# Output stage of an attention and expert kernel: projections of 64 positions, 8 KB rows for x1 and out, three variances of four on ACT

## The reference

```python
probs = jax.nn.softmax(h @ Wg, axis=-1)            # 16 experts
_, idx = jax.lax.top_k(scores, cap)                # cap = 2 of the 32 tokens at a position, per expert
hg = jnp.take_along_axis(h[:, None, :, :], idx[..., None], axis=2)
q, k, v = ...                                      # of hg, per expert, DH = 64
p = jax.nn.softmax(att, axis=1)
av = jnp.einsum('hbij,hbjd->hbid', p, v)
ao = jnp.einsum('hbid,hde->hbie', av, Wo) + bo
outs = jnp.zeros_like(t).at[b_ids, tok].add(ao)
y = t + outs
mu, var = jnp.mean(y, axis=-1), jnp.var(y, axis=-1)
yn = (y - mu) * jax.lax.rsqrt(var + 1e-05) * ln_g + ln_b
return x1 + yn
```

## Time and profile before

| | us |
|---|---|
| median of 3 runs | 1848.42 (1848.01 to 1849.35) |
| the profiled execution | 1850.22 |
| its span, first to last instruction | 1848.4 |
| busy in the span: PE, DVE, POOL, ACT | 1628.8, 1423.9, 1262.8, 1138.2 |
| output stage on DVE, first addition to last finish | 1457.0 to 1841.8 |
| DMA in and out of the output stage | 1 MB each way for each group |

### The profile page before, as it was taken

The page is one execution under the profiler, slowest core; times in us unless marked ns, Lnnn a source line. Parts: engine busy times, 40 slices in busy tenths (PEclk is TensorE's granted clock), DMA queues, the critical chain, the costliest instruction groups (busy, mean ns, idle before and its releaser), DMA issues. The chain is left out here.

```text
span 1848.4 us, 60029 instructions
## 1 busy us (share of the span) xinstructions
PE 1628.8 (88%) x22957; PEld 1335.7 (72%) x23085; DVE 1423.9 (77%) x3039; ACT 1138.2 (62%) x2758; POOL 1262.8 (68%) x1235
## 2 busy tenths in 40 slices
PE   4899999999999999999999986899997998888993
PEld 3777777777777777777777774899996765556661
DVE  2578788788787787787787877587755399999998
ACT  3677777777777777777777764223322566656662
POOL 1577776776777767767777776578872468776664
PEclk9899999999999999999999998899998799989997
DMA  6122323232232322323222112745653167776886
GB/s 213 52 89 94 99 88 105 88 99 93 93 99 88 103 90 91 102 88 105 88 93 99 48 37 76 253 133 158 199 145 75 34 164 168 171 183 152 196 197 164
DMA packets 106603, 217.83 MB, mean 118 GB/s; under 512 B 13136, under 2 KB 14544, under 8 KB 105552
## 3 DMA queue, kind: packets, MB, share of 16 engines
q1 hardware_dynamic: 96080, 180.42, 33.9%
q0 software_dynamic: 10240, 33.56, 6.2%
HBM read 146.82 MB, written 67.11 MB: 116 GB/s over the span
## 5 line engine op out<-in xcount | busy, mean ns | idle before, releaser
L316 POOL TENSOR_TENSOR rec_hn<-rec_hn,rec_out_w 128x512 f32<-128x512 f32 x128 | 199.5, 1559 | 180.3 <-DVE rec_hn L743 180.3
L294 POOL TENSOR_TENSOR rec_hrs<-rec_harg,rec_minus_half 128x8 f32<-128x8 f32 x128 | 253.8, 1983 | 10.0
L1309 POOL TENSOR_TENSOR out_x_half<-out_x_half,ln_b 128x512 f32<-128x512 f32 x128 | 158.6, 1271 | 117.7 <-DVE out_z_half L1461 117.7
L1409 PE MATMUL out_z_ps<-out_ao,out_hot 128*128 128x512 f32 x256 | 149.5, 668 | 49.3 <-DVE out_z_half L1461 43.7
L1004 PE MATMUL exp_q_ps<-exp_wqkv,exp_rows_t 128*128 128x192 f32 x1024 | 178.1, 327 | 0.1
L709 DVE TENSOR_TENSOR rec_c<-rec_s_ps,rec_d 128x512 f32<-128x512 f32 x256 | 164.7, 685 | 16.4 <-PE rec_s_ps L424 16.4
L540 ACT ACTIVATE rec_d<-rec_l_ps 128x512 f32<-128x512 f32 x256 | 150.4, 587 | 41.5 <-PE rec_l_ps L448 41.1
L1004 PEld LDWEIGHTS exp_q_ps<-exp_wqkv,exp_rows_t 128*128 128x128 f32 x1024 | 166.4, 191 | 0.7 <-ACT exp_rows_t L1058 0.3
L1058 ACT ACTIVATE exp_rows_t<-exp_t_ps 128x512 f32<-128x512 f32 x128 | 69.4, 594 | 157.3 <-PE exp_t_ps L992 132.2
L955 POOL DMA_INDIRECT exp_x_rows<-x_scratch,rowid x128 | 135.0, 1055 | 45.3 <-issue 26.1
L763 DVE TENSOR_TENSOR rec_x_ring<-rec_x_ring,rec_hn 128x512 f32<-128x512 f32 x128 | 88.6, 692 | 100.2 <-POOL rec_hn L316 99.8
(11 more groups left out here) (204 smaller groups left out, 4443.5 us busy)
## 6 DMA issues: line engine op xcount, KB each, us to landing
rec_x_ring<-in_x SPq DMA_DIRECT2D x128, 256.0 KB, 2.7
rec_ctx_ring<-in_ctx SPq DMA_DIRECT2D x128, 256.0 KB, 2.9
x_scratch<-rec_x_ring SPq DMA_DIRECT2D x128, 256.0 KB, 2.0
out_x_half<-x_scratch SPq DMA_DIRECT2D x128, 256.0 KB, 5.6
out<-out_x_half SPq DMA_DIRECT2D x128, 256.0 KB, 3.8
exp_wqkv<-in_wqkv SPq DMA_DIRECT2D x4, 1536.0 KB, 7.4
exp_x_rows<-x_scratch,rowid POOLq DMA_INDIRECT x128
wo<-in_wo SPq DMA_DIRECT2D x1, 2048.0 KB
```

The costliest lines, as they stand in the source:

```text
L294: nc.gpsimd.tensor_tensor(hrs[:, G % 2], harg[:, G % 2], mhalf[:], ALU.pow).then_inc(hrs_done, 1)
L316: nc.gpsimd.tensor_tensor(h, h, w8[:], ALU.mult).then_inc(hw_done, 1)
L1309: nc.gpsimd.tensor_tensor(xt[H % XR][:, q, :], xt[H % XR][:, q, :], lb[:], ALU.add).then_inc(xb_done, 1)
L1409: nc.tensor.matmul(z_ps[T % 3][:], hot[T % 4][:], ao[T % 4][:], start=True, stop=True).then_inc(z_full, 1)
```

## The change

- A projection piece covers 64 positions and half of the heads (`POS = 64`, pieces (k, g)): 8 matmuls of 128 columns instead of 16 of 64. `aot` holds 64 positions. `LEAD` grows from 10 to 18, so nine pieces stand ahead of the first rows. `z_ps` lends its banks to four of the first eight pieces instead of two.
- Positions in a group are numbered (b j t), t fastest: a partition's four tiles are 8 KB in one piece in DRAM. The transposes of av write their columns in that order (a step of 4 columns), and `by_row` reads the identity so.
- Of the four tiles in a group, three (`ON_ACT = 3`) get their sum with the addition (scalar_tensor_tensor with accumulating output, L1496 of the changed kernel), two small DVE operations make the mean (L1503, L1504), and ACT makes the variance: Square with accumulating output over (mean - z)/sqrt(E), L1378. The fourth tile keeps bn_stats and bn_aggr.
- On DVE the scalings of group H move behind the additions of H + 1, ahead of finish(H). z gets two buffers (`ZR = 2`), `ao` lives in the memory of `probs_all`.
- POOL waits for the squares before variance + eps; attend parts stand one group earlier, with two of them in group 0.

The diff, cut to its core:

```diff
-    NBLK = z.S // 32
+    POS = 64
+    PIECES = 2 * KC * z.S // POS
     TILES = z.S // 4
     HALVES = TILES // 4
-    XR, ZR, LEAD = 4, 3, 10
+    XR, ZR, LEAD, ON_ACT = 4, 2, 18, 3
...
-    aot = [sb(f"ao_t{p}", [P, KC, 32, 2 * NE]) for p in range(2)]
-    ao = [sb(f"ao{p}", [P, E]) for p in range(4)]
+    aot = [sb(f"ao_t{p}", [P, KC, POS, 2 * NE]) for p in range(2)]
+    ao = [spare[:, p].rearrange("p h b -> p (h b)") for p in range(4)]
...
     zt = [sb(f"z_half{r}", [P, 4, E]) for r in range(ZR)]
+    dump = sb("squares", [P, E])
+    sums = [sb(f"sums{r}", [P, ON_ACT]) for r in range(2)]
+    offs = [sb(f"offsets{r}", [P, ON_ACT]) for r in range(2)]
...
-    x_view = x1_dram.rearrange("n (b t j) e -> b j n t e", t=4, j=4)
-    o_view = out.rearrange("n (b t j) e -> b j n t e", t=4, j=4)
+    x_view = x1_dram.rearrange("n (b j t) e -> b j n t e", t=4, j=4)
+    o_view = out.rearrange("n (b j t) e -> b j n t e", t=4, j=4)
...
-            pool.wait_ge(agg_done, 4 * H + 4)
+            pool.wait_ge(agg_done, (4 - ON_ACT) * (H + 1))
+            pool.wait_ge(square_done, ON_ACT * (H + 1))
             nc.gpsimd.tensor_tensor(ve[H % 2][:], agg[H % 2][:, :, 1], epsv[:, 4 * H:4 * H + 4], ALU.add).then_inc(ve_done, 1)
             nc.gpsimd.tensor_tensor(rs[H % 2][:], ve[H % 2][:], mhalf[:], ALU.pow).then_inc(rs_done, 1)
-            c, n = divmod(H + 2, 8)
+            c, n = divmod(H + 3, 8)
+            if H == 0:
+                attend(1, 2)
             if n < 4 and c + 1 < NC:
                 attend(c + 1, n)
...
     def projected(u):
-        return z_ps if u in (1, 3) else p_ps
+        return z_ps if u < 8 and u % 2 else p_ps
...
         def put_projection(u):
-            B, k = divmod(u, 4)
+            S, piece = divmod(u, 8)
+            k, g = divmod(piece, 2)
             act.wait_ge(p_full, u + 1)
-            if B >= 2:
-                act.wait_ge(r_full, 8 * (B - 1))
+            if S >= 2:
+                act.wait_ge(r_full, 16 * (S - 1))
             for e in range(2):
-                nc.scalar.activation(aot[B % 2][:, k].rearrange("p b (h e i) -> p b h e i", e=2, i=2)[:, :, :, e, :],
-                                     projected(u)[e][:].rearrange("p (h i b) -> p b h i", i=2, b=32), ACT.Identity,
-                                     bias=bo[:, k:k + 1]).then_inc(p_read, 1)
+                nc.scalar.activation(
+                    aot[S % 2][:, k].rearrange("p b (h e i) -> p b h e i", e=2, i=2)[:, :, 4 * g:4 * g + 4, e, :],
+                    projected(u)[e][:].rearrange("p (h i b) -> p b h i", i=2, b=POS), ACT.Identity,
+                    bias=bo[:, k:k + 1]).then_inc(p_read, 1)
...
+        def deviations(H):
+            for q in range(ON_ACT):
+                act.wait_ge(mean_done, H + 1)
+                if H or q:
+                    act.wait_ge(square_done, ON_ACT * H + q)
+                nc.scalar.activation(dump[:], zt[H % ZR][:, q, :], ACT.Square, bias=offs[H % 2][:, q:q + 1],
+                                     scale=-E ** -0.5, accum_out=agg[H % 2][:, q, 1:2]).then_inc(square_done, 1)
...
         for T in range(-LEAD, TILES):
-            if T % 2 == 0 and T + LEAD < 8 * NBLK:
+            if T > 0 and T % 4 == 0:
+                deviations(T // 4 - 1)
+            if T % 2 == 0 and T + LEAD < 2 * PIECES:
                 put_projection((T + LEAD) // 2)
             if 0 <= T + 2 < TILES:
                 put_rows(T + 2)
-            if T >= 0 and T % 32 in (4, 8, 12, 16) and T // 32 + 1 < NC:
-                put_sums(4 * (T // 32 + 1) + T % 32 // 4 - 1)
+            if T >= 0 and T % 32 in (0, 4, 8, 12) and T // 32 + 1 < NC:
+                put_sums(4 * (T // 32 + 1) + T % 32 // 4)
             if 0 <= T + 4 < TILES:
                 mark(T + 4)
+        deviations(HALVES - 1)
...
-                mm = nc.tensor.transpose(t_ps[:, m * P:(m + 1) * P],
+                by_tile = t_ps[:, m * P:(m + 1) * P].rearrange("p (b t j) -> p b j t", t=4, j=4)
+                mm = nc.tensor.transpose(by_tile,
                                          av[k % 2][:, 2 * m:2 * m + 2, :].rearrange("p h d -> p (h d)"), ident[:])
             mm.then_inc(at_full, 1)
         def project(u):
-            B, k = divmod(u, 4)
-            c, b = divmod(B, 4)
+            S, piece = divmod(u, 8)
+            k, g = divmod(piece, 2)
+            c, b = divmod(S, 2)
             if u % 16 == 0:
                 pe.wait_ge(at_read, 4 * (c + 1))
-            after(pe, p_read, 2 * (u - 1) if u < 4 else 2 * u)
-            for hp in range(HP):
+            after(pe, p_read, 2 * (u - 1) if u < 8 else 2 * u)
+            for hp in range(4 * g, 4 * g + 4):
                 for e in range(2):
                     r = slice(DH * e, DH * (e + 1))
-                    mm = nc.tensor.matmul(projected(u)[e][:, 64 * hp:64 * hp + 64], wo[r, hp, P * k:P * k + P],
-                                          avt[c % 2][r, hp, :, 32 * b:32 * b + 32], start=True, stop=True)
+                    o = (hp - 4 * g) * P
+                    mm = nc.tensor.matmul(projected(u)[e][:, o:o + P], wo[r, hp, P * k:P * k + P],
+                                          avt[c % 2][r, hp, :, POS * b:POS * b + POS], start=True, stop=True)
             mm.then_inc(p_full, 1)
...
-            if T % 2 == 0 and T + LEAD < 8 * NBLK:
+            if T % 2 == 0 and T + LEAD < 2 * PIECES:
-            if T >= 0 and T % 32 in (4, 8, 12, 16) and T // 32 + 1 < NC:
-                sums_by_head(4 * (T // 32 + 1) + T % 32 // 4 - 1)
+            if T >= 0 and T % 32 in (0, 4, 8, 12) and T // 32 + 1 < NC:
+                sums_by_head(4 * (T // 32 + 1) + T % 32 // 4)
...
+        def scale(H):
+            dve.wait_ge(agg_done, (4 - ON_ACT) * (H + 1))
+            dve.wait_ge(mean_link, H + 1)
+            dve.wait_ge(square_done, ON_ACT * (H + 1))
+            for q in range(4):
+                vec.scalar_tensor_tensor(zt[H % ZR][:, q, :], zt[H % ZR][:, q, :], agg[H % 2][:, q, 0:1], lg[:],
+                                         ALU.subtract, ALU.mult).then_inc(zg_done, 1)
+
...
-                vec.tensor_tensor(zt[H % ZR][:, q, :], z_ps[T % 3][:], xt[H % XR][:, q, :], ALU.add).then_inc(z_read, 1)
-            for q in range(4):
+                if q < ON_ACT:
+                    vec.scalar_tensor_tensor(zt[H % ZR][:, q, :], z_ps[T % 3][:], 1.0, xt[H % XR][:, q, :], ALU.mult, ALU.add,
+                                             accum_out=sums[s][:, q:q + 1]).then_inc(z_read, 1)
+                else:
+                    vec.tensor_tensor(zt[H % ZR][:, q, :], z_ps[T % 3][:], xt[H % XR][:, q, :], ALU.add).then_inc(z_read, 1)
+            dve.wait_ge(z_read, 4 * H + ON_ACT)
+            if H >= 2:
+                dve.wait_ge(square_done, ON_ACT * (H - 1))
+            vec.tensor_scalar(offs[s][:], sums[s][:], E ** -1.5, None, ALU.mult).then_inc(mean_done, 1)
+            vec.tensor_scalar(agg[s][:, 0:ON_ACT, 0], sums[s][:], 1.0 / E, None, ALU.mult).then_inc(mean_link, 1)
+            for q in range(ON_ACT, 4):
                 dve.wait_ge(z_read, 4 * H + q + 1)
                 vec.bn_stats(stat[s][:, q, :], zt[H % ZR][:, q, :]).then_inc(stat_done, 1)
-            for q in range(4):
-                dve.wait_ge(stat_done, 4 * H + q + 1)
+            for q in range(ON_ACT, 4):
+                dve.wait_ge(stat_done, (4 - ON_ACT) * H + q - ON_ACT + 1)
                 vec.bn_aggr(agg[s][:, q, :], stat[s][:, q, :]).then_inc(agg_done, 1)
             if H:
+                scale(H - 1)
                 finish(H - 1)
-            dve.wait_ge(agg_done, 4 * H + 4)
-            for q in range(4):
-                vec.scalar_tensor_tensor(zt[H % ZR][:, q, :], zt[H % ZR][:, q, :], agg[s][:, q, 0:1], lg[:],
-                                         ALU.subtract, ALU.mult).then_inc(zg_done, 1)
+        scale(HALVES - 1)
         finish(HALVES - 1)
```

20 lines of the change are left out of this document (11 added, 9 removed).

## The result

| | before | changed |
|---|---|---|
| median, us | 1849.99 (12 runs) | 1844.9 (12 runs) |
| ratio | | 0.997, interval 0.9957 to 0.9983 |
| the profiled execution | 1850.22 | 1843.14 |
| its span | 1848.4 | 1841.3 |

The change makes the kernel 0.3% faster, a little under half of the 0.64% that was forecast. 1844.9 lies in the range and 8.3 us above the point. A second measurement of the same kernel gave 0.9985.

The account below looks back on a forecast made before the run. DVE sets the output stage's pace, afterwards together with the wait for x1 loads. Group intervals -13.3, tail +1.8, last stores -0.3: -11.8 us, 1850.22 to 1838.4, as a median 1836.6; range 1815 to 1856.

Parts of the forecast that it names:

- like aggregates: DVE, each group: two new operations on 128x3 would cost 0.07 to 0.15 us each, +0.2 together.
- Plain groups, 11.2: Output stage groups without an attend: period 11.2 us from (10.7 + 11.7)/2, against 10.83 before.
- D: DVE's own work in a plain group: 10.83 before, forecast 10.7 us, range 9.6 to 12.8.
- L: From the end of a finish through four stores and four x1 loads to landing: taken as 11.7 us.
- rows of 8 KB would change nothing: x1 loads: data and 32 partitions per transfer set the time, so longer rows would not shorten L.
- rival 1: x1 loads get fast, L at most 10.7, plain groups at D = 10.7: 1826 us; chance 0.17.
- even, give or take 2: Start of output stage: nine projections instead of five before the first scatter, each about half the time; no net change.
- Groups 0 and 1, 23.5: First two groups: two tiles take 4.3 instead of 5.1 and group 0 has no scaling; 23.5 against 30.3 us.
- Attend groups, 12.3: Eight groups with a POOL attend: 3.9 + 5.3 + 2.6 collision, plus slow scatter; 12.3 against 13.76 us.
- PE's speed-up hidden: PE: 0.84 us saved twice per group by shorter projections becomes idle time, except at the start.
- Rival 4: ACT becomes the bound with squares at 1.37 us each, groups 12.1: 1856 us; chance 0.08.
- rival 3: DVE additions with sums run at the contended rate, 1.31 us each, D = 12.4: 1876 us; chance 0.08.

Follow-up runs that it names:

- early_no_lnb: Changed kernel with loads for group H+3 issued ahead of the finish wait and stores, and POOL's four ln_b additions per group left out (output lacks ln_b); ratio 0.9727.
- early_loads: Changed kernel with SP issuing the loads for group H+3 ahead of the wait for group H's finish and its stores; ratio 0.9956.
- after_rows2k: Changed kernel with rows of 2 KB again, 64-position projections and variance on ACT kept; ratio to before 1.0015.
- early_means_act: Changed kernel with loads ahead of stores and the two small DVE operations on 128x3 given to ACT; ratio 0.9968.
- early_pe_sum: Changed kernel with loads ahead of stores and each attend's two products added in PSUM by PE instead of POOL's third operation; ratio 0.9958.

## Why the prediction was wrong, point by point

Against the 421.4 us of the changed stage the forecast had some 11 us less: 8.1 in the attend groups, 5.9 in groups 0 and 1, 1.2 in the plain ones and 0.5 in tail and stores, less 4.8 which it did not see at the start.

The step that failed is the price of POOL beside DVE. Two small operations were taken "like aggregates", at +0.2. They cost 0.70 in a plain group and 0.89 on average in an attend group, because one of them waits for the end of POOL's operation. In groups 0 and 1, for which the prediction gives no sum, 23.5 leaves no room for the 4.2 us of collision that the trace has there. The forecast gain of 13.3 us in the 31 intervals between groups did not come: they take 372.3 us against 370.4, 1.9 more. That the kernel is faster all the same, as forecast, is luck: within the stage it owes this to the start, which the prediction called even.

- **Plain groups, 11.2**: measured 11.26, but not by the sum it stood on, so the agreement is luck. D was to be 10.7 and is 11.04. By its terms: statistics and aggregates -2.0, measured -1.83, as 0.17 of waiting between them came back; additions with sums +0.25, measured +0.03; two small operations +0.2, measured +0.70; scalings and finishing operations, collision and waits together, +0.75 and a part of 0.3, measured +1.31; a slow PE +0.4, measured 0 (PE's clock is 1.00 in the earlier trace rows's stretch and in this one's). The term furthest off is "like aggregates": the small operation was priced by one that had met no contention. early_no_lnb shows it at 0.16 without POOL. And (D + L)/2 with the measured D would be 11.4, a wait of 0.7 in every second group; the trace has nine of 0.5 on average.
- **The loads**: the loop of finish, four stores, four loads and landing binds as told, and early_loads takes it out. L was to be 11.7. Two groups with a wait in one take 22.7 to 22.9, less D = 11.04 makes 11.7 to 11.8. But the step "rows of 8 KB would change nothing" is wrong: after_rows2k has landings of 5.7 for 5.1 and loses 0.3 to 0.45%. I had reasoned from the rate alone; the size of the pieces counts in the way of a single load. The transfers run at 240 GB/s in a full stretch, near the 228 of the earlier trace rows and under the 260 forecast, so the rate was right and rival 1 did not come. Both are above the 218 GB/s that the prediction cites for one range of 32 partitions.
- **Start of the stage, "even, give or take 2"**: 4.8 less. It priced nine pieces against five at one level of the clock; the pieces of the changed kernel reach the upper level from the fourth on (2.08, 1.92 and 2.02, then 1.12).
- **Groups 0 and 1, 23.5**: 29.4. The pace of the additions was right (group 0 takes 8.5, two tiles 4.3). But scale(0) and finish(0) stand in group 1 behind its last addition, with no wait of PE to hide in. And POOL, behind with two attends, runs beside both: in group 1 they take 6.15 and 3.53, against 2.74 each where POOL leaves them alone, 4.2 of it collision. Before had three such sets of four in these two groups (3.57, 3.32 and 5.35) with 4.0 of collision; one set is gone, the collision is not. Group 1 is 9.2 of additions at PE's pace, 1.8 of small operations and statistic, and 9.9 of these two.
- **Attend groups, 12.3**: 13.31. The groups alternate: one has scalings of 3.94 and finishing operations of 5.36, the next 2.92 and 4.34 and a fourth addition that comes 1.0 late. The collision in the first is 3.8 us and in the next 1.8, on average 2.8, where 2.6 was taken: that term was nearly right. Of the 1.0 us that is missing, 0.45 lies ahead of the scalings, where the small operations take 0.89 for 0.2. Some 0.2 is collision. The rest are the two sets' own durations and the waits between them (5.48 + 0.23, where 5.3 was taken). The late fourth addition was foreseen.
- **PE's speed-up hidden**: right in the plain groups, and PE's idle time is what let the sums go to PE.
- **ACT, "under 11.2, by little"**: squares 0.91 apart and 9.9 of 11.0, as told. Rival 4 did not bind, but it stands right behind DVE: early_means_act ran into it. The rival had allowed ACT 0.5 us of waiting for PE; there it waits 1.15 and 0.28 in one group.
- **Strided transposes**: 273 ns for a pass in the changed kernel and in before. The Trainium skill, "PSUM — Partial Sum Buffer", section "Specifications (TRN2)", says that non-contiguous patterns slow matmuls significantly; for this step of four columns the measurement differs, and it decides.
- **Slow additions with sums (rival 3)**: 0.614 apart with 0.08 for reading the sum. The Trainium skill, "Vector Engine (DVE) Microarchitecture Reference", section "Points that are easy to get wrong", speaks of two SBUF sources; with one in PSUM the rows show no slowing.

Why the change gains so little inside the groups follows from these runs. The statistics that it takes from DVE have one SBUF input. They were the time in which POOL's additions could run without hurting (2.46 in the earlier trace rows, beside POOL's 4.96). Without them the scalings, with two SBUF inputs, move under POOL's work and give back 1.3 of the 1.83, and the small operations the rest and more. early_means_act shows the same again: 0.56 us less of DVE's work ahead of the scalings, and the scalings 0.56 longer. In the loads' loop the new order costs a further 0.2. What stays is the 64-position projection.

Open: why the small operations wait for POOL's operation and the statistic does not (it is not the form of the output), why PE regains its clock with long passes, and where the 2.5 to 4 us lie by which the medians favour the change more than the stage does.

## What to carry to other kernels

Before moving an operation off DVE, look at what POOL does during it: an operation with one SBUF input can be the cover for POOL's work, and its removal then gains nothing. Price a collision by counting POOL's operations that lie beside DVE's two-input ones. Here it paid to take work from POOL and not from DVE: one POOL operation less per attend made the attend groups 0.5 to 1.1 us shorter, three statistics less on DVE made its plain group 0.2 longer. And when two engines hand work back and forth, price the loop with its waits, at the clock that the waits leave.

## What the runs showed of the hardware

- DVE's operations with two SBUF inputs and POOL's go side by side one for one: a scaling takes 1.54 to 1.76 instead of 0.74, POOL's operation 1.39 to 1.73 instead of 1.06 to 1.27. One POOL operation less gave DVE 1.00 back (5.34 to 4.34).
- A DVE operation on 128x3 takes 0.16 alone. With one of POOL's 128x512 operations under way it ends 0.02 to 0.03 us behind that one, so it takes up to 1.24. The next one right behind it mostly takes 0.15.
- An ACT square with its sum takes 0.91 instead of 0.72; the same on DVE costs 0.08, which the next operation hides.
- Five projections of 32 passes of 64 columns at the start of the stage all ran at the lower clock (3.6 to 3.7 each); of nine with 16 passes of 128 columns only the first three did, and none of the nine in early_pe_sum.
- Rows of 8 KB over 32 partitions move hardly faster in a full stretch (240 GB/s at a DMA share of 1.01, against 228 at 0.89), yet single loads land 0.6 us sooner.
